# The fill of a two-attention pipeline, written out as an order of its own

## Chip, core, metric

The kernel runs on 1 core of one Trainium2 chip. The metric is the device time of one execution in microseconds; three executions are timed, and a fourth is profiled.

## What is computed

Eight images of 32 x 32 tokens with 256 channels pass through two residual attention blocks, each behind a group normalisation over 32 groups of channels:

```python
def reference(x, w_qkv, w_proj, b_proj, Wq, Wk, Wv, gamma):
    ...
    x = x + _L0_conv_ref(_gn(x), L0_conv_w_qkv, L0_conv_w_proj, L0_conv_b_proj)
    x = x + _L1_conv_ref(_gn(x), L1_conv_Wq, L1_conv_Wk, L1_conv_Wv, L1_conv_gamma)
    return x
```

`_L0_conv_ref` is attention inside windows of 32 tokens with 8 heads of width 32, then a 256 x 256 projection and a bias. `_L1_conv_ref` is attention over all 1024 tokens of an image, with `energy = k q^T` of inner width 32, a softmax over the keys, and `gamma * (attn v)`.

## The kernel before

The first block is called the local stage (names that begin with `a_`), the second the global stage (`b_`). Products that need more than half precision are made of three float16 matmuls (`split3`, lines 253 to 255), so weights and activations exist as a high and a low part (`a_nh` and `a_nl`, `b_nh` and `b_nl`, `v_h` and `v_l`).

Each engine has one program, written by hand in the order in which it runs, and semaphores join them. `pa` is four PSUM banks of 512 floats for the local stage, `pb` four banks for the global stage. A step `i` of the pipeline has two halves, `first(i, b, o, m, f)` and `second(i, b, o, m, f)`. The flags say which image's work exists: `f` is the front of the local stage of image i+2, `m` the rest of the local stage of image i+1, `b` the global attention of image i, `o` the output of image i-1. The program runs `first(-2)`, `second(-2)`, then `all_steps`, which runs the steps from -1 up, with steps 2 to 4 as a loop.

The local stage of one image goes like this. The image is loaded (`load`) and turned by TensorE (`transposes`), ScalarE copies it out (`copy_T`), VectorE takes statistics (`stats`), TensorE averages over groups (`group_mean`, `group_var`), GpSimd makes the factors (`rstd`), ScalarE and GpSimd make `a_nh` and `a_nl`. TensorE projects q and k (`a_project_qk`) and v (`a_project_v`). SyncE spreads k onto the diagonal of `diag` by 8 DMAs (`k_spread`, line 333). TensorE makes scores (`a_scores`); VectorE subtracts maxima (`a_maximum`, lines 874 and 879), ScalarE exponentiates (`a_exponential`, line 714), VectorE sums rows (`a_row_sum`, lines 884 and 886), GpSimd multiplies (`a_probabilities`, line 1083), VectorE turns blocks (`a_transpose`, line 892), SyncE spreads them into the same `diag` by 8 DMAs (`p_spread`, line 343), and TensorE makes the outputs (`a_output`, line 491). ScalarE and VectorE split them into `before_turn` (`a_out_high`, `a_out_low`, line 896), SyncE regroups that by 16 DMAs (`a_regroup`, line 321), and TensorE projects (`a_projection`); VectorE adds the result to the image (`a_residual`, line 905) and so has `x1`.

The global stage of an image turns `x1`, normalises it (`b_norm_split` on VectorE, lines 860 and 862), projects q and k, and copies them into `q_stack` and `k_stack` by 4 DMAs (`b_stacks`, lines 307 to 310). For each of 8 row tiles TensorE makes an energy (`b_energy`, line 539) and VectorE a maximum (`b_maximum`, line 925). With all maxima split (`b_max_split`, line 932), the second half `second(i)` makes the transposed energies (`b_energy_T`, line 557), their exponentials (line 749) and the value projection (`b_project_v`, `b_v_high`, `b_v_low`), between the matmuls of the local stage of image i+2 and the end of that of image i+1. The weights are scaled at the start: a maximum of each matrix, a turn and a sum on TensorE (lines 656 and 658), then `weights_high` and `weights_low`.

An engine runs strictly in its written order: what stands behind a waiting instruction waits too. The DMAs of SyncE stand in one such order as well.

## Time and profile before

| what | value |
|---|---|
| time, median of 3 | 690.84 us (688.51 to 690.97) |
| the profiled execution's own time | 689.47 us |
| its span | 687.7 us |
| TensorE busy | 593.7 us (86%) |
| VectorE busy | 473.2 us (69%) |
| ScalarE busy | 349.5 us (51%) |
| GpSimd busy | 196.9 us (29%) |
| mean granted TensorE clock | 0.945 |

The span is the time from the first to the last instruction of the profiled execution; what lies around it, 1.8 us here, is in the time too. Times within the trace are counted from the span's start. The granted clock is given as a share of full speed: 1.00 is 2.4 GHz and 0.50 is 1.2 GHz.

### The profile page before, as it was taken

How to read it: one execution, taken by the hardware profiler on the slowest of the kernel's cores; microseconds unless marked ns; L12 is line 12 of the kernel's file. 1: busy time of each engine (PE TensorE's matmuls, PEld its weight loads, DVE VectorE, ACT ScalarE, POOL GpSimd, SP SyncE). 2: the span in 40 equal slices, each digit the busy share in tenths (PEclk: the TensorE clock that was granted, in tenths of full speed). 3: DMA queues.
4: the chain of work that ended last, by engine and by line, in shares of the span. 5: the costliest groups of instructions: out<-in, count | busy, mean ns of one | idle time of the engine just before them, and what ended most of it. 6: DMA issues, size and time to landing. Idle time of an engine off the chain costs nothing.

```text
span 687.7 us, 15145 instructions
## 1 busy us (share of the span) xinstructions
PE 593.7 (86%) x5859; PEld 429.9 (63%) x5859; DVE 473.2 (69%) x765; ACT 349.5 (51%) x486; POOL 196.9 (29%) x194
## 2 busy tenths in 40 slices
PE   2475587689999999999999999999999999649987
PEld 2254265346877677757775777668776767327756
DVE  4445246868886878687868788688868794664562
ACT  2522425097518852686348652875278513651363
POOL 5602221132046023513342314420460342001203
PEclk9795798599999999999999999999999999879999
DMA  5042132212332332243042323224223132201101
GB/s 160 0 124 62 43 83 82 62 38 64 108 74 66 78 93 71 63 108 93 23 107 76 84 61 92 68 57 112 68 68 82 33 74 64 72 1 39 49 0 62
DMA packets 40308, 47.53 MB, mean 69 GB/s; under 512 B 6848, under 2 KB 32320, under 8 KB 40256
## 3 DMA queue, kind: packets, MB, share of 16 engines
q1 hardware_dynamic: 36960, 43.47, 24.0%
q10 hardware_dynamic: 3296, 3.34, 1.4%
q8 instruction: 35, 0.57, 0.4%
q14 instruction: 17, 0.14, 0.1%
HBM read 10.09 MB, written 8.39 MB: 27 GB/s over the span
## 4 chain that ended last, share of the span: by engine, by line
PE 64%; DVE 16%; ACT 6%; issue 5%; SPq 4%; DMA 3%; POOL 1%; ACTq 0%; DVEq 0%; POOLq 0%
PE pb L253 9%; PE pb L254 8%; PE pb L255 8%; PE pa L253 7%; PE pa L255 6%; PE pa L254 6%; PE pa L491 4%; DVE max_neg L925 4%; PE pb L557 4%; PE pa L464 3%; PE pb L539 3%; SPq L321 3%; DVE ast L827 2%; PE pa L393 2%; PE pb L393 2%
## 5 line engine op out<-in xcount | busy, mean ns | idle before, releaser
L253 PE MATMUL pb<-v_h,e_h 128*128 128x257 f16 x464 | 127.5, 275 | 0.0
L255 PE MATMUL pb<-v_h,e_l 128*128 128x257 f16 x464 | 126.5, 273 | 0.0
L254 PE MATMUL pb<-v_l,e_h 128*128 128x257 f16 x464 | 126.1, 272 | 0.0
L925 DVE TENSOR_REDUCE max_neg<-pb 128x1 f32<-128x1024 f32 x64 | 77.5, 1211 | 55.6 <-PE pb L539 55.1
L940 DVE TENSOR_TENSOR e_l<-e,e_h 128x1024 f16<-128x1024 f32 x64 | 77.8, 1223 | 17.1 <-ACT e L749 15.5
L758 ACT ACTIVATE qk_h<-pb,y_fac 128x256 f32<-128x256 f32 x58 | 27.5, 474 | 109.9 <-DVE y_fac L947 109.6
L1097 POOL TENSOR_TENSOR y<-qk_h,y 128x256 f32<-128x256 f32 x64 | 46.3, 727 | 118.1 <-ACT qk_h L758 118.0
L749 ACT ACTIVATE e<-pb,f_energy 128x1024 f32<-128x1024 f32 x64 | 71.3, 1114 | 16.1 <-PE pb L557 16.1
L1078 POOL TENSOR_TENSOR xb<-xin,bias 128x2048 f32<-128x2048 f32 x8 | 36.7, 4588 | 125.9 <-DVE x L905 125.9
L1083 POOL TENSOR_TENSOR before_turn<-before_turn,a_rinv 128x1024 f32<-128x1024 f32 x16 | 30.6, 1912 | 128.3 <-DVE a_rinv L886 128.3
L253 PE MATMUL pa<-a_nh,wqkv_h 128*128 128x512 f16 x128 | 49.9, 389 | 13.1 <-DVE before_turn L896 7.3
L748 ACT ACTIVATE e_h<-pb,f_energy 128x1024 f16<-128x1024 f32 x40 | 44.5, 1113 | 20.2 <-PE pb L557 20.1
L253 PEld LDWEIGHTS pb<-v_h,e_h 128*128 128x128 f16 x464 | 45.7, 99 | 13.7 <-issue 1.7
L254 PEld LDWEIGHTS pb<-v_l,e_h 128*128 128x128 f16 x464 | 45.7, 98 | 11.9
L539 PE MATMUL pb<-q_stack,k_stack 96*128 96x512 f16 x128 | 40.4, 398 | 14.2 <-DVE max_neg L925 12.8
L693 ACT ACTIVATE a_nh<-a_xT,anb,ar 128x512 f16<-128x512 f32 x32 | 25.7, 803 | 48.2 <-POOL anb L1060 48.2
L254 PE MATMUL pa<-a_nl,wqkv_h 128*128 128x512 f16 x128 | 49.7, 388 | 0.0
L255 PE MATMUL pa<-a_nh,wqkv_l 128*128 128x512 f16 x128 | 49.5, 387 | 0.0
L255 PEld LDWEIGHTS pb<-v_h,e_l 128*128 128x128 f16 x464 | 44.7, 96 | 6.9
L557 PE MATMUL pb<-k_stack,q_stack 98*128 98x512 f16 x128 | 38.9, 385 | 10.9 <-ACT e L749 9.5
L1071 POOL TENSOR_TENSOR a_nl<-a_xT,a_nh 128x512 f16<-128x512 f32 x32 | 37.1, 1158 | 18.7 <-ACT a_xT L695 18.7
L253 PE MATMUL pa<-wp_h,turned 128*128 128x256 f16 x128 | 35.9, 281 | 2.3 <-DMA turned<-before_turn 2.3
(136 smaller groups left out, 1373.4 us busy)
## 6 DMA issues: line engine op xcount, KB each, us to landing
xin<-in_x SPq DMA_DIRECT2D x16, 512.0 KB, 4.6
diag<-qkT SPq DMA_DIRECT2D x64, 128.0 KB, 2.3
diag<-turned SPq DMA_DIRECT2D x64, 128.0 KB, 2.4
turned<-before_turn SPq DMA_DIRECT2D x128, 64.0 KB, 2.0
out<-y SPq DMA_DIRECT2D x24, 256.0 KB, 2.1
out<-y ACTq DMA_DIRECT2D x8, 256.0 KB, 2.1
q_stack<-qk_hl SPq DMA_DIRECT2D x8, 128.0 KB, 2.3
k_stack<-qk_hl SPq DMA_DIRECT2D x8, 128.0 KB, 2.4
```

What stands on the lines that cost most here:

```text
L253: nc.tensor.matmul(out_ap, lh, rh, start=start, stop=False)
L254: nc.tensor.matmul(out_ap, lh, rl, start=False, stop=False)
L255: return nc.tensor.matmul(out_ap, ll, rh, start=False, stop=stop)
L539: last = nc.tensor.matmul(pb[:, c, :], k_stack[0:96, it * P:(it + 1) * P], q_stack[0:96, c * CHUNK:(c + 1) * CHUNK], start=True, stop=True)
L557: last = nc.tensor.matmul(pb[:, c, :], q_stack[0:98, jt * P:(jt + 1) * P], k_stack[0:98, c * CHUNK:(c + 1) * CHUNK], start=True, stop=True)
L748: nc.scalar.activation(e_h[:, jt, :], src, ACT.Exp, scale=f_energy[:, 0:1])
L749: nc.scalar.activation(e32[:, jt % 2, :], src, ACT.Exp, scale=f_energy[:, 0:1]).then_inc(b_exp, 1)
L925: nc.vector.tensor_reduce(max_neg[:, it:it + 1], pb[:, 0:2, :].rearrange("p a n -> p (a n)"), X, ALU.max, negate=True).then_inc(b_max, 1)
L940: nc.vector.tensor_tensor(e_l[:, jt, :], e32[:, jt % 2, :], e_h[:, jt, :], ALU.subtract).then_inc(b_el, 1)
L1071: nc.gpsimd.tensor_tensor(a_nl[:, ct, cols], a_xT[:, ct, cols], a_nh[:, ct, cols], ALU.subtract).then_inc(n_["a"]["nl"], 1)
L1078: nc.gpsimd.tensor_tensor(xb[:], xin[:], bias[:].unsqueeze(1).broadcast_to([P, TILES, CH]), ALU.add).then_inc(a_xb, 1)
L1097: nc.gpsimd.tensor_tensor(y[:, it, :], y_part[:, it % 2, :], y[:, it, :], ALU.add).then_inc(b_y, 1)
```

## The change

The fill, that is all work up to the maxima of image 0's energies, is no longer `first(-2)`, `second(-2)`, `first(-1)`, `second(-1)` and `first(0)`, but a list of its own on each engine. `all_steps` then begins with `second(0)`. In the new list

- image 0 is loaded ahead of `w_proj` and the global stage's weights on SyncE's queue, and it is turned ahead of the weights' maxima on TensorE;
- image 1 is turned through banks 2 and 3 of `pb` (`turn_bank`), and its group means and variances stand there (`group_bank`), so that it can be turned while image 0's scores are not yet done; its q, k, v and scores stand between the stages of image 0;
- image 0's projection goes to `pb` (`proj_bank`);
- the value projection of image 0's global stage, with its high and low parts, stands ahead of and between the first energies and no longer in `second(0)`;
- `memset` of `diag` comes first on GpSimd, and the small ones later.

```diff
-            for i in range(-1, 2):
-                peeled(first, i)
-                peeled(second, i)
+            peeled(second, 0)
+            peeled(first, 1)
+            peeled(second, 1)
...
+        def turn_bank(k, b, j):
+
+            return pa[:, j, :] if k == "a" and not image(b, 1) else pb[:, 2 + j % 2, :]
+
+        def group_bank(k, b, which):
+
+            if k == "b":
+                return pb[:, 2 + which, 0:CT]
+            return pb[:, 2 + which, 384:384 + CT] if image(b, 1) else pa[:, 1 + 2 * which, 384:384 + CT]
+
+        def proj_bank(b, j):
+
+            return pb[:, 2 + j % 2, :] if image(b, 0) else pa[:, 2 + j % 2, :]
...
+            load(0)
             sp.dma_start(wp_f, w_proj.rearrange("(a p) n -> p a n", p=P)).then_inc(s_wp, 16)
...
-            load(0)
-            sp.wait_ge(s_pool, 6)
-            second(-2, False, False, False, True)
+            load(1)
+            sp.wait_ge(s_pool, 2)
+            sp.nop(nofuse=True)
+            k_spread(0, 0)
+            k_spread(0, 1)
+            p_spread(0, 0)
+            p_spread(0, 1)
+            k_spread(1, 0)
+            k_spread(1, 1)
+            a_regroup(0)
+            load(2)
+            p_spread(1, 0)
+            p_spread(1, 1)
+            b_stacks(0)
             all_steps(sp, first, second)
...
+            transposes("a", 0, range(4))
+            group_mean("a", 0)
             pe.wait_ge(s_wmax, 1)
...
+            group_var("a", 0)
...
-            first(-2, False, False, False, True)
 
             pe.wait_ge(s_ready, 1)
-            second(-2, False, False, False, True)
+            a_project_qk(0, 0, range(4))
+            transposes("a", 1, (0, 1))
+            a_project_qk(0, 1, (0, 1))
+            transposes("a", 1, (2, 3))
+            a_project_qk(0, 1, (2, 3))
+            a_project_v(0, (0, 1))
+            group_mean("a", 1)
+            a_project_v(0, (2, 3))
+            group_var("a", 1)
+            a_scores(0)
+            a_project_qk(1, 0, range(4))
+            a_project_qk(1, 1, range(4))
+            a_output(0, True, 0)
+            a_output(0, True, 1)
+            a_project_v(1, range(4))
+            a_scores(1)
...
+            a_projection(0, True, range(4))
+            transposes("b", 0, range(4))
+            group_mean("b", 0)
+            group_var("b", 0)
...
+            for c in range(CHUNKS):
+                b_project_qk(0, True, c)
+            transposes("a", 2, range(4))
+            b_project_v(0, (0, 1))
+            b_energy(0, 0, True)
+            b_project_v(0, (2,))
+            b_energy(0, 1, True)
+            b_project_v(0, (3,))
+            b_energy(0, 2, True)
+            group_mean("a", 2)
+            a_output(1, True, 0)
+            b_energy(0, 3, True)
+            group_var("a", 2)
+            a_output(1, True, 1)
+            for it in range(4, 8):
+                b_energy(0, it, True)
...
             def second(i, b, o, m, f):
-                if b: b_project_v(i, (0,))
+                if b and not image(i, 0): b_project_v(i, (0,))
                 if b: b_max_rows(i)
...
+            a_exponential(0, 0)
+            a_exponential(0, 1)
...
+            a_exponential(1, 0)
+            copy_T("b", 0, range(4))
+            normalise("b", 0)
+            a_exponential(1, 1)
+            b_qk_high(0)
...
+            weight_maximum(slice(0, 1))
+            stats("a", 0)
+            weight_maximum(slice(1, 5)).then_inc(s_wmax, 1)
...
+            a_residual(0, range(4))
+            a_maximum(1, 1)
+            stats("b", 0)
+            group_mean("b", 0)
+            a_row_sum(1, 0)
+            group_scale("b", 0)
+            a_row_sum(1, 1)
+            b_norm_split(0)
+            a_transpose(1, 0)
+            a_transpose(1, 1)
+            b_qk_low(0)
...
```

Three places of the order are needed later. The first is VectorE, from the variance of image 0's global normalisation (`be`, `bve`) to its high and low parts. Before the change:

```order
L845 TENSOR_TENSOR be<-be,bmv 128x2 [waits bn_sq]
L850 TENSOR_SCALAR bve<-pb 128x2 [waits bn_gv]
L860 CAST b_nh<-b_xT 128x512 [waits bn_xn]
L862 TENSOR_TENSOR b_nl<-b_xT,b_nh 128x512 [waits bn_nh]
...
L874 TENSOR_REDUCE a_rmax<-pa 128x32 [waits a_s]
L879 TENSOR_TENSOR before_turn<-pa,a_rmax 128x1024 [waits a_ox,a_max]
L914 SCALAR_TENSOR_TENSOR qk_hl<-qk_h,masks,pb 128x512 [waits b_qkh] x2
```

With the change:

```order
L948 TENSOR_TENSOR be<-be,bmv 128x2 [waits bn_sq]
L987 TENSOR_REDUCE a_rsum<-before_turn 128x32 [waits a_exp]
L989 RECIPROCAL a_rinv<-a_rsum 128x32 [waits a_sum]
L953 TENSOR_SCALAR bve<-pb 128x2 [waits bn_gv]
L987 TENSOR_REDUCE a_rsum<-before_turn 128x32 [waits a_exp]
L989 RECIPROCAL a_rinv<-a_rsum 128x32 [waits a_sum]
L963 CAST b_nh<-b_xT 128x512 [waits bn_xn]
L965 TENSOR_TENSOR b_nl<-b_xT,b_nh 128x512 [waits bn_nh]
...
L995 STREAM_TRANSPOSE turned<-before_turn 128x1024 [waits a_y,a_prob] x2
L1017 SCALAR_TENSOR_TENSOR qk_hl<-qk_h,masks,pb 128x512 [waits b_qkh] x2
```

Image 1's two row sums (`a_rsum`) moved ahead of the split of image 0's normalised tokens, and its two block turns (`turned`) stand between that split and `qk_hl`.

The second is ScalarE over the same stretch, from the copies of the turned `x1` (`b_xT<-pb`) on. Before:

```order
L680 ACTIVATE b_xT<-pb 128x512 [waits bn_tr] x4
L710 ACTIVATE v_tok<-pb 128x512 [waits a_o,a_v] x3
L695 ACTIVATE b_xT<-b_xT,bnb,br 128x512 [waits bn_nb]
L695 ACTIVATE b_xT<-b_xT,bnb,br 128x512
...
L729 ACTIVATE qk_h<-pb 128x512 [waits b_qk] x2
L714 ACTIVATE before_turn<-before_turn 128x1024 [waits a_sub] x2
```

With the change:

```order
L795 ACTIVATE before_turn<-before_turn 128x1024 [waits a_sub]
L761 ACTIVATE b_xT<-pb 128x512 [waits bn_tr] x4
L776 ACTIVATE b_xT<-b_xT,bnb,br 128x512 [waits bn_nb]
L776 ACTIVATE b_xT<-b_xT,bnb,br 128x512 x3
L795 ACTIVATE before_turn<-before_turn 128x1024 [waits a_sub]
L810 ACTIVATE qk_h<-pb 128x512 [waits b_qk] x2
```

Image 1's second exponential (`before_turn<-before_turn`) moved from behind `qk_h` to between the normalisation of image 0 and `qk_h`.

The third is SyncE's queue, from the regrouping of image 0 (`turned<-before_turn`) to that of image 1; `diag<-qkT` is a k spread, `diag<-turned` a spread of probabilities. Before:

```order
L321 DMA turned<-before_turn 32x2x512 [waits a_ol]
L321 DMA turned<-before_turn 32x2x512 x15
L333 DMA diag<-qkT 32x2x512 [waits a_ke,a_o]
...
L297 DMA xin<-in_x 128x4x256 [waits an_tr,a_xb] x2
L307 DMA q_stack<-qk_hl 64x1024 [waits b_qkl]
L308 DMA k_stack<-qk_hl 64x1024
L309 DMA q_stack<-qk_hl 32x1024
L310 DMA k_stack<-qk_hl 32x1024
L343 DMA diag<-turned 32x1024 [waits a_pt,a_s]
```

With the change:

```order
L338 DMA turned<-before_turn 32x2x512 [waits a_ol]
L338 DMA turned<-before_turn 32x2x512 x15
L314 DMA xin<-in_x 128x4x256 [waits an_tr,a_xb] x2
L360 DMA diag<-turned 32x1024 [waits a_pt,a_s]
L360 DMA diag<-turned 32x1024 x3
L360 DMA diag<-turned 32x1024 [waits a_pt,a_s]
L360 DMA diag<-turned 32x1024 x3
L324 DMA q_stack<-qk_hl 64x1024 [waits b_qkl]
L325 DMA k_stack<-qk_hl 64x1024
L326 DMA q_stack<-qk_hl 32x1024
L327 DMA k_stack<-qk_hl 32x1024
```

The 8 k spreads of image 1 went ahead of the regrouping of image 0, and the 8 spreads of image 1's probabilities went from behind the 4 stack transfers to ahead of them.

## Rows read from the trace of the kernel before

**Rows 1.** Windows: length, busy of PE, PEld, DVE, ACT, POOL, clock, DMA.

```profile
116.00:150.00 34.00, 24.21 (x221) 15.10 (x222) 23.11 (x32) 15.52 (x21) 11.57 (x12) 0.71 0.18 42
150.00:190.00 40.00, 39.31 (x386) 28.45 (x385) 32.32 (x49) 26.92 (x38) 6.65 (x4) 1.00 0.33 87
```

**Rows 2.** Chain of waits that ended last: start, length, what.

```profile
3.52 6.83 DMA gam<-in_L_conv_gamma
...
87.15 1.99 DMA turned<-before_turn
```

**Rows 3.** Timeline, ScalarE: start, length, instruction, idle before it.

```profile
22.43 0.81 ACT L693 ACTIVATE a_nh<-a_xT,anb,ar 128x512 f16<-128x512 f32 x1 [5.79 <-POOL anb L1060]
...
106.47 1.51 ACT L695 ACTIVATE b_xT<-b_xT,bnb,br 128x512 f32<-128x512 f32 x2
...
115.89 1.06 ACT L714 ACTIVATE before_turn<-before_turn 128x1024 f32<-128x1024 f32 x1 [2.63 <-DVE before_turn L879]
```

**Rows 4.** Timeline, TensorE.

```profile
26.80 0.59 PE L253 MATMUL pa<-a_nh,wqkv_h 128*128 128x512 f16 x1 [5.76 <-POOL a_nl L1071]
...
45.20 3.70 PE L464 MATMUL pa<-diag,qkT 128*32 128x128 f32 x128 [0.99 <-DMA diag<-qkT]
...
89.18 0.28 PE L253 MATMUL pa<-wp_h,turned 128*128 128x256 f16 x1 [2.06 <-DMA turned<-before_turn]
...
97.89 1.04 PE L393 MATMUL pb<-ident,x 128*128 128x128 f32 x8
...
119.44 1.06 PE L539 MATMUL pb<-q_stack,k_stack 96*128 96x512 f16 x2
...
131.35 3.64 PE L491 MATMUL pa<-diag,v_tok 128*32 128x128 f32 x64
...
136.57 1.96 PE L491 MATMUL pa<-diag,v_tok 128*32 128x128 f32 x64 [0.57 <-DMA diag<-turned]
...
140.47 0.59 PE L539 MATMUL pb<-q_stack,k_stack 96*128 96x512 f16 x2 [1.41 <-DVE max_neg L925]
...
145.92 0.60 PE L557 MATMUL pb<-k_stack,q_stack 98*128 98x512 f16 x2 [1.10 <-ACT k_stack L740]
...
158.80 0.60 PE L557 MATMUL pb<-k_stack,q_stack 98*128 98x512 f16 x2
```

**Rows 5.** Timeline, VectorE.

```profile
95.57 0.75 DVE L905 SCALAR_TENSOR_TENSOR x<-pa,f_proj,xb 128x512 f32<-128x512 f32 x1 [1.50 <-PE pa L255]
...
102.76 0.16 DVE L850 TENSOR_SCALAR bve<-pb 128x2 f32<-128x2 f32 x1 [0.70 <-PE pb L405]
...
109.07 0.69 DVE L862 TENSOR_TENSOR b_nl<-b_xT,b_nh 128x512 f16<-128x512 f32 x1
...
114.63 1.22 DVE L879 TENSOR_TENSOR before_turn<-pa,a_rmax 128x1024 f32<-128x1024 f32 x1
115.78 1.21 DVE L884 TENSOR_REDUCE a_rsum<-before_turn 128x32 f32<-128x1024 f32 x1
117.02 0.35 DVE L886 RECIPROCAL a_rinv<-a_rsum 128x32 f32<-128x32 f32 x1
...
142.57 0.17 DVE L932 SCALAR_TENSOR_TENSOR max_hl<-max_neg,max_hl 128x8 f16<-128x8 f32 x1
...
146.11 1.21 DVE L896 TENSOR_TENSOR before_turn<-pa,before_turn 128x1024 f16<-128x1024 f32 x1
```

**Rows 6.** Timeline, SyncE's queue: issues.

```profile
56.99 5.04 SPq L343 DMA_DIRECT2D diag<-turned  x8
77.51 10.23 SPq L321 DMA_DIRECT2D turned<-before_turn  x16
...
115.73 0.59 SPq L310 DMA_DIRECT2D k_stack<-qk_hl  x1
```

**Rows 7.** Timeline, GpSimd and VectorE at the same time.

```profile
193.35 1.91 POOL L1083 TENSOR_TENSOR before_turn<-before_turn,a_rinv 128x1024 f32<-128x1024 f32 x1 [1.97 <-DVE a_rinv L886]
...
194.45 0.82 DVE L947 TENSOR_TENSOR y_fac<-y_inv,f_out 128x1 f32<-128x1 f32 x1
```

177 lines of the change are left out of this document (125 added, 52 removed).

## The prediction, made blind

> **What bounds the kernel now.** I read the windows first, then the chain of waits, then the timelines of the engines up to 190 us. From 150 us on TensorE is busy 39.31 of 40 us at full clock [rows 1], so there the kernel is bound by TensorE and an offset gained or lost before is carried to the end. From 116 to 150 us it is busy 24.21 of 34 us at a mean clock of 0.71 [rows 1]: there, and earlier, latency bounds it. The change rewrites just this part, so the question is when TensorE reaches a place from which its work is the same in both programs. I take the projection of image 1 (`a_projection(1)`): before, TensorE comes to it when the sixth transposed energy is done, at 158.80 + 0.45 = 159.25 us [rows 4], and its input has landed by then, at about 159.1 us: the low part of the outputs ends at 147.32 us [rows 5], then 16 DMAs are issued and the last lands, 11.7 us together (from 77.51 [rows 6] to 89.18 [rows 4]).
>
> **The new order, walked in steps.** Each step below adds durations of rows; "before" is the same event in the trace.
>
> *Start.* TensorE's first instruction waits for the last constant, at 3.52 + 6.83 = 10.35 us [rows 2]; the first projection comes at 26.80 us [rows 4]. The image loaded first does not lift this gate, and its turn and the weights' scale still share one chain: VectorE now has four weight maxima behind the image's statistics and ahead of the scale. I take the length from gate to projection as it was (16.45 us; bounds 2 less and 2 more). But 1 MB of image now stands ahead in the DMA engines; I add 0.9 us (bounds 0 and 2.8). First projection: 27.7 us.
> The Trainium skill, "DMA: Bandwidth & Descriptors", section on queues, rings and completion order, says that each DMA engine takes turns between the queues that have work; the constants are on another queue than the image, so by this rule nothing would be added, and by a strict first come, first served all of the image's transfer. No run here shows which.
>
> *Image 0's scores.* Image 1 is turned between the projections: 2 x 1.04 us [rows 4]. Scores start at 45.20 + 0.9 + 2.1 = 48.2 (before 45.20).
>
> *Image 0's local attention.* First half of the scores at 50.05; maxima and differences 4 x 1.21 (as the rows of lines 879 and 884 [rows 5]) to 55.0. The exponentials, 1.06 us each [rows 3], stand behind image 1's normalisation on ScalarE (8 x 0.71, from 49.2) and so start at 54.9. Two row sums with reciprocals, 1.56 each [rows 5], to 59.1; two k copies of image 1 (1.35, as two other copies of their kind) to 60.4; two block turns 2.5 to 62.9. The spread of probabilities, 8 issues in 5.04 us [rows 6], starts at 61.7 behind the first turn, its last DMA lands at 68.6, and half the outputs takes 1.96 us at high clock or 3.64 at low [rows 4]. TensorE has worked until 2.3 us before, so I take 1.96: 70.5 us.
>
> *Regrouping.* The queue now issues image 1's 8 k spreads first, 5.04 us, to 75.6. High and low part of the outputs (1.91 + 2.4 us) are hidden by that. Regrouping starts at 75.65 (before 77.51 [rows 6]): 1.9 sooner. The projection of image 0: 87.3 (before 89.18 [rows 4]).
>
> *x1.* TensorE has idled 6 us and starts at low clock, which costs about 1.6 us on 48 matmuls of 0.11; the last residual ends at 95.0 (before 95.57 + 0.75 = 96.3 [rows 5]): 1.3 sooner. Image 1's projections, values and scores are already behind us here; their work is what the change takes off this stretch.
>
> *Variance of the global norm.* Now VectorE does image 1's second maximum and difference first (2.4, to 97.4), then statistics (2.85), the averages (1.3, four VectorE products of 2 columns and two small matmuls), then a row sum of 1.56, and only then `bve`: 103.2 (before 102.92 [rows 5]). The gain is gone.
>
> *Its high and low parts.* Factors 1.05, four normalisations of 0.75 (two in 1.51 [rows 3]) to 107.3. `b_norm_split` stands behind image 1's second row sum, which waits for an exponential that ScalarE runs only behind that normalisation: 1.06 + 1.56 to 109.9. At that moment GpSimd starts its product of 1.92 us. In the rows a VectorE product of 128x1, else 0.16 us, took 0.82, from 194.45 to 195.27, and the GpSimd product beside it ran from 193.35 to 195.26 [rows 7]: VectorE was held until GpSimd ended. I take it that casts and differences with two SBUF inputs are held alike: 1.5 us (bounds 0 and 1.9). End of the split: 115.7 (before 109.07 + 0.69 = 109.76 [rows 5]): 5.9 later.
> The Trainium skill, "SBUF — State Buffer", section on the two separate sides, calls the shared port pair an exclusive lock held for a whole instruction; by it a cast that comes first would instead hold GpSimd, for 0.4 us. The trace agrees as far as the one row goes.
>
> *First energy.* Before, 109.76 to 119.44 [rows 4]. Now image 1's block turns come first on VectorE (2.45), and on SyncE's queue 8 spreads stand ahead of the 4 stack transfers. The spreads start at 116.95 and occupy the queue for 5.04 us [rows 6] to 122.0; the last of the stack issues starts 1.85 later and lands in 2.0 (before: issued at 115.73 [rows 6]). First energy: 126.0, 6.6 later. `qk_hl` is ready at 119.5 and waits.
>
> *Energies to the split maxima.* Before 119.44 to 142.74 [rows 4, 5], 23.3 us, much at low clock. Between the maxima VectorE now has two `v_l` (1.4), half the statistics (1.6) and the group mean (0.8), no longer row sum and block turns. With a cycle of 2.0 us at high clock (0.59 + 1.41 [rows 4]) and the waits for both output halves it comes to 20.6 us; with energies of 1.06 and output halves of 3.64 [rows 4] to 27. The value projections keep TensorE busy for some microseconds at the start of it, so I take 22.0: split maxima at 148.0 (before 142.74), 5.3 later.
>
> *Second half, step 0.* Before, the first transposed energy came 3.2 us behind the split, since v copies and the output's high part stood ahead of the row copy on ScalarE; now 1.8: 149.8 (before 145.92 [rows 4]), 3.9 later. Of the four value projections taken out (1.31 us each, 5.2 together), two lay in that wait, one lies under an exponential (1.11 twice), and one, 1.3 us, was in TensorE's own path. So the sixth transposed energy ends 11.9 us on, at 161.7. The regrouping of image 1: low parts end at 150.45, all landed 11.7 later, 162.2. This is later than TensorE. `a_projection(1)`: 162.2 against 159.25, **2.9 us later**. From there both programs do the same, bound by TensorE, so 2.9 us is what is left at the end.
>
> Other moves cost nothing: `diag` cleared first on GpSimd ends before the constants land; the small memsets lie under ScalarE's copies; image 2's load ends 20 us before its turn.
>
> **Sum.** 689.47 (the profiled execution) + 2.9 = 692.4. The profiled execution lies 1.4 us under the median of the three timed ones (690.84); the mean of all four is 690.0, and I set the forecast against that: 690.0 + 2.9 = 692.9. What a measurement of this kernel can tell from no change is about 0.5%, 3.45 us.
>
> **Rivals.**
> *The energies run at low clock* (0.2). For: the clock of this stretch before, 0.71 [rows 1], and now a wait of 4 us for the stack transfers ahead of it. Price: 27 instead of 22 us, +5, and +1.7 if image 0's output half is slow too: 695 to 700.
> *The steps cancel* (0.17). The constants land as before (-0.9), the GpSimd product holds nothing (-1.5), the stretch runs at high clock (-1.4): -0.9 in all, 689.1. Against: all three have to hold.
> *The maxima hide VectorE's other work* (0.13), the faster side. If `v_l`, statistics and averages fit into the 1.4 us in which VectorE waits in each cycle, energies to split is 8 x 2.0 + 0.5 = 16.5 us, the split comes at 142.5, the regrouping lands at 156.7, and TensorE arrives at 156.2: -2.6, and with the constants unmoved -3.5, 686.5. It decides from a stretch under 18.5 us. Against: three waits for TensorE's averages and output halves stand in that stretch in written order.
> *Image first does take the gate away*: an earlier first constant would shift all by as much; the gate's own DMA is untouched, so I give it a part of the last rival only.
>
> **How the numbers follow.** Forecast (offset of +1 to +5, 691 to 695): 0.5. Of it 40% lie above 3.45 us. Slower by over 0.5%: 0.2 + 0.2 = 0.40. Faster by over 0.5%: 0.13, the last rival with room for a step that I overlooked. The same: 0.47. Range: from 687.5, between the two rivals below, to 698, in the low clock's; about 0.1 lies outside on each side. The likeliest one's own range is 691 to 695.
>
> **What would show it.** In the new trace: first projection near 27.7 us; regrouping of image 0 issued near 75.7; first b_nh cast near 110, a held cast or difference beside a GpSimd product; the q and k stack DMAs issued behind 8 probability spreads, near 122; first energy near 126; split maxima near 148; TensorE waiting for `turned` ahead of image 1's projection, near 162. Wrong would be: a first energy before 121, an energies stretch under 19 us, or a clock that stays low into `second(0)`.

## The result

| | kernel before | changed kernel |
|---|---|---|
| time, median of 5 | 688.51 us (688.17 to 690.97) | 694.38 us (693.66 to 696.15) |
| ratio to before | | 1.0082, 95% interval 1.0062 to 1.0103 |
| profiled execution's own time, span | 689.47 us, 687.7 us | 696.15 us, 694.4 us |
| TensorE, VectorE busy | 593.7 us, 473.2 us | 593.8 us, 470.4 us |
| mean granted TensorE clock | 0.945 | 0.953 |

The change makes the kernel 0.8% slower. In a second comparison on another chip it was 1.0107 [1.0081, 1.0133] of before (`e10_changed_again`, below). By the medians its cost was 5.9 us in the first comparison and 7.5 us in the second. The forecast was 692.9 us, that is +2.9 us.

The windows of the changed kernel, with the columns of [rows 1]:

```profile
116.00:150.00 34.00, 23.37 (x224) 14.29 (x224) 20.20 (x31) 13.21 (x20) 7.09 (x9) 0.80 0.19 44
150.00:190.00 40.00, 36.93 (x327) 23.11 (x328) 29.34 (x45) 24.78 (x31) 6.06 (x5) 0.89 0.30 80
```

Against [rows 1] the first stretch has about as much TensorE work (23.37 against 24.21 us), at a better clock (0.80 against 0.71). The loss shows in the second: 36.93 busy of 40 us against 39.31, and a clock of 0.89 against 1.00. The stretch in which latency bounds the kernel has grown longer, past 150 us.

TensorE's timeline of the changed kernel shows where it comes to each place (start, length, instruction, idle before it and what ended that):

```profile
25.79 0.58 PE L270 MATMUL pa<-a_nh,wqkv_h 128*128 128x512 f16 x1 [6.29 <-POOL a_nl L1218]
...
88.57 0.37 PE L270 MATMUL pb<-wp_h,turned 128*128 128x256 f16 x1 [5.69 <-DMA turned<-before_turn]
...
115.93 0.59 PE L270 MATMUL pb<-b_nh,wqk_h 128*128 128x512 f16 x1 [11.61 <-DVE b_nl L965]
...
128.70 1.04 PE L583 MATMUL pb<-q_stack,k_stack 96*128 96x512 f16 x2 [2.90 <-DMA k_stack<-qk_hl]
...
146.11 1.01 PE L583 MATMUL pb<-q_stack,k_stack 96*128 96x512 f16 x2 [1.41 <-DVE max_neg L1028]
...
151.28 1.01 PE L590 MATMUL pb<-ident_h,max_hl 128*2 128x128 f16 x8 [1.73 <-DVE max_hl L1035]
153.39 1.04 PE L601 MATMUL pb<-k_stack,q_stack 98*128 98x512 f16 x2 [1.11 <-ACT k_stack L821]
...
156.78 1.06 PE L601 MATMUL pb<-k_stack,q_stack 98*128 98x512 f16 x2
...
166.43 0.61 PE L601 MATMUL pb<-k_stack,q_stack 98*128 98x512 f16 x2
```

The same places, before, predicted, and measured:

| event | before | predicted | measured |
|---|---|---|---|
| first projection | 26.80 | 27.7 | 25.79 |
| projection of image 0 (L270 <- turned) | 89.18 | 87.3 | 88.57 |
| last residual ends (`x1`) | 96.3 | 95.0 | 97.5 |
| `bve` ends | 102.92 | 103.2 | 105.4 |
| high and low parts of image 0 end | 109.76 | 115.7 | 117.8 |
| first energy | 119.44 | 126.0 | 128.70 |
| maxima split, end | 142.74 | 148.0 | 151.22 |
| first transposed energy | 145.92 | 149.8 | 153.39 |
| projection of image 1 | 159.25 | 162.2 | 166.87 |

From there the offset only travels. SyncE's regrouping of later images was issued at 219.91 and, for the last image, at 583.51 us before; in the changed kernel at 227.73 and 591.22, so +7.8 for the first of them and still +7.7 five images later. The last image's first energy comes at 632.87 against 626.03: 0.9 us is given back in the last steps, where TensorE waits again, and the span ends 6.7 us later.

VectorE of the changed kernel, over the stretch in which the offset grows:

```profile
105.32 0.10 DVE L953 TENSOR_SCALAR bve<-pb 128x2 f32<-128x2 f32 x1
110.41 1.22 DVE L987 TENSOR_REDUCE a_rsum<-before_turn 128x32 f32<-128x1024 f32 x1 [5.00 <-ACT before_turn L795]
...
111.94 0.36 DVE L963 CAST b_nh<-b_xT 128x512 f16<-128x512 f32 x1
112.34 2.27 DVE L965 TENSOR_TENSOR b_nl<-b_xT,b_nh 128x512 f16<-128x512 f32 x1
...
117.72 2.37 DVE L995 STREAM_TRANSPOSE turned<-before_turn 128x1024 f32<-128x1024 f32 x2
...
121.88 0.75 DVE L1017 SCALAR_TENSOR_TENSOR qk_hl<-qk_h,masks,pb 128x512 f16<-128x512 f16 x1 [1.17 <-ACT qk_h L810]
```

ScalarE of the changed kernel at the same time:

```profile
109.34 1.04 ACT L795 ACTIVATE before_turn<-before_turn 128x1024 f32<-128x1024 f32 x1
...
121.25 0.60 ACT L810 ACTIVATE qk_h<-pb 128x512 f16<-128x512 f32 x1 [1.96 <-PE pb L272]
```

and GpSimd:

```profile
112.10 1.96 POOL L1230 TENSOR_TENSOR before_turn<-before_turn,a_rinv 128x1024 f32<-128x1024 f32 x1 [3.76 <-DVE a_rinv L989]
```

VectorE has nothing to do for 5.00 us ahead of 110.41: it stands at the second row sum of image 1, which waits for the exponential of 109.34 that ScalarE runs behind image 0's normalisation. The first chunk of image 0 has been normalised since about 107.2, and its cast, behind that row sum, comes at 111.94. Then `b_nl` of 112.34 takes 2.27 us, where the other three take 0.69: it begins when GpSimd's product (112.10 to 114.06) already runs, and it ends 0.55 us after that product.

SyncE's queue of the changed kernel:

```profile
69.75 6.26 SPq L350 DMA_DIRECT2D diag<-qkT  x8
76.12 10.93 SPq L338 DMA_DIRECT2D turned<-before_turn  x16
...
119.50 5.17 SPq L360 DMA_DIRECT2D diag<-turned  x8
124.78 0.53 SPq L324 DMA_DIRECT2D q_stack<-qk_hl  x1
...
153.61 10.25 SPq L338 DMA_DIRECT2D turned<-before_turn  x16
```

The 8 spreads of image 1's probabilities hold the queue from 119.50 to 124.7. `qk_hl` is complete at 122.63, and its first transfer is issued at 124.78. TensorE waits 11.61 us for `b_nl` (115.93) and then 2.90 for the stacks (128.70).

### The profile page after: what moved, and what is told of

Read it like the earlier page. It is cut to its first block, busy times and chain, and to the rows that moved or that the text cites. A ratio compares the mean times of both kernels' runs of the same rounds, so it can differ in the third digit from the quotient of the medians.

```text
span 694.4 us, 15142 instructions
## 1 busy us (share of the span) xinstructions
PE 593.8 (86%) x5859; PEld 428.5 (62%) x5859; DVE 470.4 (68%) x765; ACT 349.0 (50%) x486; POOL 197.8 (28%) x194
## 4 chain that ended last, share of the span: by engine, by line
PE 65%; DVE 15%; ACT 7%; issue 5%; SPq 4%; DMA 3%; POOL 1%; ACTq 1%; DVEq 0%; POOLq 0%
PE pb L270 9%; PE pb L271 9%; PE pb L272 9%; PE pa L270 6%; PE pa L271 6%; PE pa L272 6%; PE pb L601 4%; DVE max_neg L1028 4%; PE pa L535 4%; PE pb L583 3%; PE pa L502 3%; ACT e L830 2%; PE pa L425 2%; PE pb L425 2%; DVE a_rsum L987 2%
## 5 line engine op out<-in xcount | busy, mean ns | idle before, releaser
L270 PE MATMUL pb<-v_h,e_h 128*128 128x257 f16 x464 | 127.4, 275 | 0.0
L270 PE MATMUL pa<-a_nh,wqkv_h 128*128 128x512 f16 x128 | 50.1, 391 | 9.1 <-POOL a_nl L1218 9.1
L270 PEld LDWEIGHTS pb<-v_h,e_h 128*128 128x128 f16 x464 | 45.7, 99 | 13.6 <-issue 1.4
L583 PE MATMUL pb<-q_stack,k_stack 96*128 96x512 f16 x128 | 39.5, 391 | 16.8 <-DVE max_neg L1028 12.5
L601 PE MATMUL pb<-k_stack,q_stack 98*128 98x512 f16 x128 | 40.3, 397 | 10.9 <-ACT e L830 9.5
L270 PE MATMUL pb<-wv_h,b_nh 128*128 128x256 f16 x128 | 35.6, 278 | 0.0
```

What stands on the lines that cost most here:

```text
L270: nc.tensor.matmul(out_ap, lh, rh, start=start, stop=False)
L583: last = nc.tensor.matmul(pb[:, c, :], k_stack[0:96, it * P:(it + 1) * P], q_stack[0:96, c * CHUNK:(c + 1) * CHUNK], start=True, stop=True)
L601: last = nc.tensor.matmul(pb[:, c, :], q_stack[0:98, jt * P:(jt + 1) * P], k_stack[0:98, c * CHUNK:(c + 1) * CHUNK], start=True, stop=True)
```

## The experiments

Each is the changed kernel with one edit, unless it says otherwise, and was executed 4 to 12 times. The ratio is to the kernel before on the same chip, whose medians were 689.5 to 690.1 us there (688.51 in the first comparison). The last three columns are starts on TensorE in the one profiled execution ("rows of maxima" is `b_max_rows`, which follows the split). The two traces of the unaltered changed kernel show how far one program's starts differ: 1.2 us at the first energy, but only 0.02 at the rows of maxima and 0.2 at the sixth transposed energy. These two columns tell more than the first.

| kernel | time, us | ratio [95%] | first energy | rows of maxima | sixth transposed energy |
|---|---|---|---|---|---|
| kernel before | 688.51 | 1 | 119.44 | 142.80 | 158.80 |
| changed | 694.38 | 1.0082 [1.0062, 1.0103] | 128.70 | 151.28 | 166.43 |
| the same again | 697.11 | 1.0107 [1.0081, 1.0133] | 129.88 | 151.30 | 166.22 |
| `e1_sum_late` | 697.18 | 1.0113 [1.0087, 1.0138] | 127.39 | 149.83 | 164.43 |
| `e2_stacks_first` | 695.69 | 1.0071 [1.0049, 1.0093] | 127.70 | 149.66 | 164.06 |
| `e3_both` | 689.06 | 0.9986 [0.9967, 1.0006] | 122.00 | 144.57 | 158.55 |
| `e5_turn_between` | 693.57 | 1.0055 [1.0031, 1.0078] | 127.64 | 149.67 | 164.01 |
| `e4_load_last` | 698.79 | 1.0140 [1.0108, 1.0173] | 129.43 | 150.84 | 165.60 |
| `e6_v_back` | 696.90 | 1.0104 [1.0080, 1.0129] | 128.41 | 150.68 | 165.41 |
| `e7_filler` | 693.76 | 1.0052 [1.0035, 1.0070] | 127.81 | 149.72 | 162.86 |
| `e8_chain_first` | 688.07 | 0.9972 [0.9960, 0.9983] | 118.94 | 141.99 | 156.05 |
| `e9_chain_filler` | 684.49 | 0.9936 [0.9910, 0.9961] | 117.67 | 139.40 | 152.53 |
| `e11_regroup_first` | 689.30 | 0.9997 [0.9977, 1.0017] | 118.92 | 142.68 | 157.16 |
| before, `e12_before_filler` | 687.54 | 0.9969 [0.9953, 0.9985] | 120.66 | 144.41 | 159.15 |

### Two gates ahead of the first energy: e1, e2, e3

The theory: the first energy is late because image 1's work stands ahead of image 0's at two places, the row sum on VectorE (with its exponential on ScalarE) and the spreads on SyncE's queue.

`e1_sum_late` moves the first, `e2_stacks_first` the second, `e3_both` both:

```diff
 # e1, ScalarE
-            a_exponential(1, 1)
             b_qk_high(0)
+            a_exponential(1, 1)
 # e1, VectorE
-            a_row_sum(1, 1)
             b_norm_split(0)
+            b_qk_low(0)
+            a_row_sum(1, 1)
             a_transpose(1, 0)
             a_transpose(1, 1)
-            b_qk_low(0)
 # e2, SyncE
+            b_stacks(0)
             p_spread(1, 0)
             p_spread(1, 1)
-            b_stacks(0)
```

> Image 1's second exponential and row sum stand behind qk_high and qk_low of image 0; SyncE's queue is as in the changed kernel. Theory (chain and queue together): the split of image 0's normalised tokens ends near 111.6 us instead of 117.8 and qk_hl is ready near 115.6 instead of 122.6, but the stack transfers stay behind 8 spreads of probabilities that now wait for a later row sum, so the first energy moves from 128.7 to about 128 and the time falls by under 1 us against the changed kernel (694.4). Rival (the row sum is the whole cause): the first energy at about 120 to 122 and the time 5 to 7 us lower, near 688.

> Only SyncE's queue changes: the 4 stack transfers of image 0 stand ahead of the 8 spreads of image 1's probabilities. Theory: qk_hl is ready at 122.6, so the first stack issue is at 122.7 instead of 124.8 and the first energy at about 126.6 instead of 128.7; the spreads land near 132.5, still ahead of image 1's outputs at 136.9. Time 2 us lower than the changed kernel, near 692.4. Rival (the queue is the whole cause): 5 us lower or more.

> Both edits of the two runs before. Theory: qk_hl ready near 115.6, first energy near 119.6 (before the change 119.4), that is about 9 us sooner than in the changed kernel, although the two edits alone give under 1 and 2 us; split maxima near 142.5; time 7 to 9 us below the changed kernel, 685.5 to 687.5, at or a little under the kernel before. Rival (low clock of TensorE in the stretch is what costs): the first energy moves, but the split maxima stay beyond 147 and the time above 690.

Each edit alone took 1.0 to 1.3 us off the first energy, hardly more than the 1.2 by which two traces of the changed kernel differ, and 1.8 to 2.4 us off the sixth transposed energy. Their ratios, 1.0113 and 1.0071, show no gain clear of noise: the first lies above and the second below the changed kernel's own two. Both together took 6.7 us off the first energy and 7.7 to 7.9 off the sixth transposed energy, and the time came back to that of before. It was expected under that, at 685.5 to 687.5 us, with a first energy at 119.6 and not 122.0; `e8_chain_first` below takes up what was left. The rival expected of it, rows of maxima still late at low clock, did not come about. The rows of `e1_sum_late`, SyncE and then TensorE, say why the first alone does so little:

```profile
118.34 5.02 SPq L360 DMA_DIRECT2D diag<-turned  x8
123.47 0.53 SPq L324 DMA_DIRECT2D q_stack<-qk_hl  x1
```

```profile
127.39 1.04 PE L583 MATMUL pb<-q_stack,k_stack 96*128 96x512 f16 x2 [9.56 <-DMA k_stack<-qk_hl]
```

`qk_hl` was complete at 114.89 there, 7.7 us sooner than in the changed kernel, but the stack transfers stand behind spreads that now wait for the late row sum and turns: the queue comes to them at 123.47, and TensorE waits 9.56 us. In `e2_stacks_first` the transfers go at 123.78, as soon as `qk_hl` is there (123.31), but `qk_hl` is late. In `e3_both` VectorE and the queue are both free. VectorE, and then SyncE's queue:

```profile
108.18 1.27 DVE L963 CAST b_nh<-b_xT 128x512 f16<-128x512 f32 x1 [1.95 <-ACT b_xT L776]
...
116.86 0.75 DVE L1017 SCALAR_TENSOR_TENSOR qk_hl<-qk_h,masks,pb 128x512 f16<-128x512 f16 x1 [1.22 <-ACT qk_h L810]
```

```profile
118.08 0.53 SPq L324 DMA_DIRECT2D q_stack<-qk_hl  x1
```

`qk_hl` ends at 117.61 and its first transfer goes at 118.08. VectorE's rows show the held instruction once more: the cast of 108.18 takes 1.27 us instead of 0.42, beside GpSimd's product of image 1's first half.

### The GpSimd product: e5

`e5_turn_between` puts image 1's first block turn between the second row sum and the high and low parts, so that it is the turn that runs when the product begins:

```diff
             a_row_sum(1, 1)
-            b_norm_split(0)
             a_transpose(1, 0)
+            b_norm_split(0)
             a_transpose(1, 1)
```

> Image 1's first block turn stands on VectorE between its second row sum and the split of image 0's normalised tokens, beside GpSimd's product. Theory of the lock (VectorE's casts and two-input differences are held while GpSimd's product runs, a turn is not): the turn takes its 1.2 us, and the first cast and difference together take under 2.2 us instead of 2.7; the split ends within 0.7 us of 117.8. The first four spreads leave SyncE's queue from 113.3 on and no longer block the stacks, so the first energy comes at 126.5 to 127.5 instead of 128.7; time 1 to 2 us lower than the changed kernel. Rival (no lock; the 2.27 us difference was something else): the first difference takes 2.2 us again.

VectorE of this kernel:

```profile
112.53 1.19 DVE L995 STREAM_TRANSPOSE turned<-before_turn 128x1024 f32<-128x1024 f32 x1
113.64 1.25 DVE L963 CAST b_nh<-b_xT 128x512 f16<-128x512 f32 x1
114.92 0.69 DVE L965 TENSOR_TENSOR b_nl<-b_xT,b_nh 128x512 f16<-128x512 f32 x1
```

and SyncE's queue:

```profile
114.27 9.34 SPq L360 DMA_DIRECT2D diag<-turned  x8
123.72 0.53 SPq L324 DMA_DIRECT2D q_stack<-qk_hl  x1
```

The turn is not held (1.19 us, as ever), but the cast behind it is, 1.25 instead of 0.42 us. Cast and difference together take 1.94 us, in the changed kernel 2.63, so 0.7 us of the hold is saved and 0.8 remains. The first energy came 1.1 us sooner and the sixth transposed energy 2.4; the ratio is 1.9 to 3.6 us below the changed kernel's two, with an interval that meets that of the first.

These gains are not the shorter hold's. The turn now stands ahead of the split, so the split ended at 118.80 us, 1.0 later than in the changed kernel, where I had expected it within 0.7, and `qk_hl` was complete at 123.35, 0.7 later. What came sooner is the queue: the first four spreads left from 114.27 on (the row merges them with the other four, 120.09 to 123.61), so the stack transfers went at 123.72 instead of 124.78. Of the 2.4 us at the sixth transposed energy, 0.8 are clock: the third transposed energy came 2.03 us behind the second (2.87 in the changed kernel). So the rows show a hold of about 1.5 us in the changed kernel (2.63 us against 0.42 + 0.69), a part and not the cause of the loss; what it is worth in the time, this edit does not show.

### The start and the value projections: e4, e6

`e4_load_last` moves `load(0)` back behind the weights on SyncE's queue. `e6_v_back` takes image 0's value projections, with their high and low parts, out of the fill and puts them back into `second(0)`:

```diff
 # e4, SyncE
-            load(0)
             sp.dma_start(wp_f, w_proj.rearrange("(a p) n -> p a n", p=P)).then_inc(s_wp, 16)
...
+            load(0)
 # e6, TensorE
-            b_project_v(0, (0, 1))
             b_energy(0, 0, True)
-            b_project_v(0, (2,))
             b_energy(0, 1, True)
-            b_project_v(0, (3,))
...
-                if b and not image(i, 0): b_project_v(i, (0,))
+                if b: b_project_v(i, (0,))
```

> Image 0's load goes back behind the weights on SyncE's queue, all else as changed. In the changed kernel the first turn starts at 10.38 us with the last constant, and the first projection at 25.79. Theory (the load's place is worth at most what the image lands later than the constant): the first turn starts at 11 to 12.5, the first projection at 26.5 to 28, the time 0.5 to 2 us higher. Rival (the place of the load is worth nothing, since the constant gates both): first turn at 10.4 and no change.

> The value projection of image 0's global stage and its high and low parts go back into second(0); all else as changed. Theory (moving them was worth about one microsecond): first energy unchanged near 128.7, split maxima 1 to 2 us sooner, the first transposed energy at the same distance from the split as before the change (3.2 us) instead of 2.2, the sixth transposed energy about 1.3 us further behind the first; the time within 1.5 us of the changed kernel. Rival (taking 5.2 us of TensorE work from second(0) paid in full and hid a larger loss): the time rises by 4 to 5 us, near 699.

TensorE's start in `e4_load_last`:

```profile
12.07 3.65 PE L425 MATMUL pa<-ident,xin 128*128 128x128 f32 x16 [12.07 <-DMA xin<-in_x]
...
27.45 0.58 PE L270 MATMUL pa<-a_nh,wqkv_h 128*128 128x512 f16 x1 [6.30 <-POOL a_nl L1218]
```

With the image behind the weights its turn waits for the image until 12.07 us, and the first projection comes at 27.45 instead of 25.79. So loading the image first is worth 1.7 us at its place. Whether it is worth anything at the end is open. The time rose to 1.0140, 2 to 4 us above the changed kernel, where 0.5 to 2 was expected, but its interval meets that of the changed kernel's second comparison, and the trace does not carry the delay: `x1` was there at 97.75 against 97.5, because the low clock of image 0's projection lasted 2.7 us instead of 5.7, and the sixth transposed energy came at 165.60, ahead of the changed kernel's 166.43 and 166.22. That profiled execution, at 695.16 us, was the quickest of its four.

`e6_v_back` shows both sides of the value projections. Among the energies they cost nothing that can be told: from the first energy to the rows of maxima it takes 22.27 us without them and 22.58 with them, and the rows of maxima came 0.6 us sooner where 1 to 2 was expected. In `second(0)` they lengthen the way from the first to the sixth transposed energy to 12.87 us, as before (12.88 from [rows 4]), against 13.04 in the changed kernel, where the first two steps ran at low clock. The times, 1.0104 against 1.0082 and 1.0107, do not differ: this move neither makes the loss nor hides it.

### The clock: e7

`e7_filler` adds to the changed kernel matmuls of `wqkv_h` with itself, 128x512, whose results nobody reads, in the stretches in which TensorE idles (4 more stand behind the rows of maxima, and a wait for `b_vl` ahead of the last four energies; both are left out here):

```diff
+            def filler(bank, n):
+                for _ in range(n):
+                    nc.tensor.matmul(bank, wqkv_h[:, 0, 0:P], wqkv_h[:, 0, 0:CHUNK], start=True, stop=True)
...
             a_scores(1)
+            pe.wait_ge(a_ve, 8)
+            filler(pb[:, 0, :], 24)
...
+            filler(pb[:, 0, :], 48)
             for c in range(CHUNKS):
                 b_project_qk(0, True, c)
...
+            pe.wait_ge(b_qkl, 2)
+            filler(pb[:, 0, :], 24)
             b_energy(0, 0, True)
...
             for it in range(4, 8):
                 b_energy(0, it, True)
+                filler(pb[:, 2, :], 4)
```

> The changed kernel with TensorE matmuls added whose results nobody reads, in its idle stretches: 24 ahead of image 0's projection, 48 ahead of the projection to global q and k, 24 ahead of the first energy, 4 behind each of the last four energies and behind the rows of maxima. Theory (the low clock costs a part of the loss): granted clock near 1.00 from 84 us on; last residual of image 0 ends about 2 us sooner, the last three energy cycles take 2.0 instead of 2.4 us, the first transposed energies 2.8 and 1.8 apart instead of 3.4 and 2.9; the time 3 to 6 us below the changed kernel. Rival (low clock is covered by other waits): under 1 us. If the added matmuls are too many and delay a step, its start shows it.

The windows of this kernel, with the columns of [rows 1]:

```profile
110.00:120.00 10.00, 10.00 (x60) 5.83 (x59) 9.32 (x13) 2.94 (x6) 1.96 (x1) 1.00 0.12 27
...
150.00:160.00 10.00, 9.11 (x45) 3.50 (x43) 6.21 (x6) 7.54 (x9) 0.00 (x0) 1.00 0.28 70
```

The clock is 1.00 from 110 to 120 and from 150 to 160 us, where the changed kernel had 0.50 and 0.55. `qk_hl` was there at 119.5 us instead of 122.6, but the queue still stood at the spreads, so the first energy came only 0.9 us sooner. The last stack transfer was issued 2.0 us sooner (124.62 against 126.62) but took 3.15 us to land instead of 2.03. The energies and the first transposed energies then gained 2.7 us more (sixth at 162.86). The time is 1.0052, 2 to 4 us under the changed kernel by the ratios, with an interval that meets that of the first comparison; 3 to 6 us were expected. Low clock is thus a part of the loss, 3.6 us at the sixth transposed energy where the order of `e3_both` is worth 7.9, and what it gains ahead of the first energy is hidden as long as the queue is the gate.

### Image 0's chain first: e8

`e8_chain_first` is `e3_both` with two more of image 1's operations moved behind image 0's:

```diff
             a_residual(0, range(4))
-            a_maximum(1, 1)
             stats("b", 0)
             group_mean("b", 0)
-            a_row_sum(1, 0)
             group_scale("b", 0)
+            a_maximum(1, 1)
             b_norm_split(0)
+            a_row_sum(1, 0)
             b_qk_low(0)
```

> As the run with both edits, and on VectorE image 1's second maximum stands behind the variance of image 0's global norm, its first row sum behind the split of the normalised tokens. Theory (what stands in image 0's chain is late by what it takes, 2.4 and 1.5 us): variance near 103.3 instead of 106.1, first cast 0.4 us instead of 1.27 since no GpSimd product runs beside it, first energy near 119 instead of 122.0; time 2 to 3 us below the run with both edits, near 686. Rival (the chain is held elsewhere, by TensorE's turns and clock): no change against it.

TensorE of this kernel:

```profile
118.94 0.61 PE L583 MATMUL pb<-q_stack,k_stack 96*128 96x512 f16 x2 [1.33 <-DMA k_stack<-qk_hl]
...
156.05 0.60 PE L601 MATMUL pb<-k_stack,q_stack 98*128 98x512 f16 x2
...
157.78 0.28 PE L270 MATMUL pa<-wp_h,turned 128*128 128x256 f16 x1 [1.13 <-DMA turned<-before_turn]
```

`bve` started at 102.89 us, 3.3 sooner than in `e3_both` (106.14) and 2.4 sooner than in the changed kernel (105.32), the first cast was not held (0.42 us), and the first energy came at 118.94, 3.1 us before that of `e3_both` and 9.8 before the changed kernel's. The time is 0.9972 [0.9960, 0.9983], faster than before. Here TensorE does wait for the regrouping ahead of image 1's projection, 1.13 us: the wait that I had forecast for the changed kernel appears when TensorE is early enough.

### The new order again, with the clock held, and one step more: e10, e9, e11

`e10_changed_again` is the changed kernel unaltered. `e9_chain_filler` is `e8_chain_first` with extra matmuls at the places of `e7_filler`, 22, 20, 18 and 4 (the last behind each of the last four energies and behind the rows of maxima; its expectation names that place wrongly). `e11_regroup_first` is `e8_chain_first` with image 1's k spreads behind image 0's regrouping, and what hangs on them moved back:

```diff
 # e11, SyncE
+            a_regroup(0)
             k_spread(1, 0)
             k_spread(1, 1)
-            a_regroup(0)
 # e11, TensorE
-            a_scores(1)
...
             group_var("b", 0)
+            a_scores(1)
```

> The changed kernel once more, so that it stands beside the two next ones on one chip. Expected: a ratio of 1.007 to 1.009 to the kernel before, as measured first (1.0082), so about 5.5 us above it, and 6 to 7.5 us above the level of the order that moves image 1's work behind image 0's (688.07 us when it was measured). If that order's gain was the chip's and not the order's, the distance here is under 4 us.

> The order that moves image 1's work behind image 0's and puts the stack transfers first, plus TensorE matmuls of which nobody uses the result, in the stretches in which it idles (22 ahead of image 0's variance, 20 ahead of the first low part, 18 ahead of the first energy, 4 ahead of image 0's projection quarters). Theory that low clock still costs in this fill: the first energy comes at about 117.5 us instead of 118.9, the first three transposed energies are 2.8 and 1.8 us apart, and the time is 0.5 to 2 us under that order's own level of about 688 us; it is held to that because the regrouped outputs of image 1 land at about 158.5 and TensorE's wait for them, 1.1 us, grows. Rival, that only latencies of VectorE, ScalarE and DMA bound the fill: the same time within 0.5 us, or longer, because the added matmuls stand in front of real ones.

> The same order, and moreover the regrouping of image 0 stands ahead of the k spreads of image 1 on SyncE's queue, with all that hangs on those spreads moved back: image 1's scores behind image 0's variance on TensorE, its maxima, exponentials and row sums one place later on VectorE and ScalarE. Theory, that each microsecond taken off image 0's chain ahead of the first energy is a microsecond off the time as long as image 1's own chain is covered: the regrouping starts at about 74 us instead of 77.0, image 0's projection comes at 86.5, bve at about 100.4, the first energy at about 116.5, and the time is 1 to 2.5 us under that order's level, about 686 us. Rival, that image 1's chain is then the later one: its outputs wait for its spreads by more than 2 us among the energies, its regrouping lands as late as before, the wait of TensorE ahead of image 1's projection grows to about 3 us, and the time stays at 688.

The distance from `e9_chain_filler` to the changed kernel, on one chip, is 12.6 us. The extra matmuls gave more than expected. TensorE in `e9_chain_filler`:

```profile
82.16 4.92 PE L701 MATMUL pb<-wqkv_h 128*128 128x512 f16 x22
89.20 0.27 PE L270 MATMUL pb<-wp_h,turned 128*128 128x256 f16 x1 [2.12 <-DMA turned<-before_turn]
...
100.83 6.16 PE L701 MATMUL pb<-wqkv_h 128*128 128x512 f16 x20
...
117.67 0.60 PE L583 MATMUL pb<-q_stack,k_stack 96*128 96x512 f16 x2
...
152.53 0.61 PE L601 MATMUL pb<-k_stack,q_stack 98*128 98x512 f16 x2
153.40 0.28 PE L270 MATMUL pa<-wp_h,turned 128*128 128x256 f16 x1 [0.27 <-DMA turned<-before_turn]
```

Image 0's projection now starts at full clock (0.27 us a matmul from the first one), `bve` came at 101.01 against 102.89, the first energy 1.3 us sooner, the rows of maxima 2.6 and the sixth transposed energy 3.5; the spans differ by 4.6 us. I had expected the regrouping to hold it back, but the low part of the outputs stands behind the split on VectorE and moved with it: the regrouping was issued at 141.72 instead of 144.32, and TensorE waited 0.27 us (153.40).

The counts are not the best ones. The first low part of image 0 was ready at 104.62 us, but TensorE was at the 20 extra matmuls until 107.0. The last stack transfer, issued at 113.33, landed at about 115.4 (2.0 us), but TensorE stood at the 18 extra matmuls (113.79) until the first energy at 117.67. So in both places matmuls that nobody reads held real ones, by 2.4 and about 2.2 us. No run has fewer of them.

`e11_regroup_first` started the regrouping at 74.72 and image 0's projection at 86.47, as expected; the first energy was to come at 116.5 and came at 118.92. TensorE of this kernel:

```profile
86.47 0.37 PE L270 MATMUL pb<-wp_h,turned 128*128 128x256 f16 x1 [10.88 <-DMA turned<-before_turn]
...
100.48 5.37 PE L502 MATMUL pa<-diag,qkT 128*32 128x128 f32 x128
```

and VectorE of the same kernel:

```profile
103.59 1.23 DVE L977 TENSOR_REDUCE a_rmax<-pa 128x32 f32<-128x1024 f32 x1 [2.99 <-PE pa L502]
...
105.99 0.42 DVE L963 CAST b_nh<-b_xT 128x512 f16<-128x512 f32 x1
```

Image 1's scores, now at 100.48, ran 5.37 us at low clock instead of 3.70, and VectorE's maximum of image 1 (103.59), which stands ahead of the first cast, waited 2.99 us for them: the 2.5 us won at `bve` (100.44) were lost there, to 105.99 against 105.36. This is the changed kernel's fault in small: work of image 1 ahead of a ready instruction of image 0. The ratio is 0.9997, 1.7 us behind `e8_chain_first` by the ratios, with intervals that just meet; 1 to 2.5 us ahead of it was expected. The rival named for it, outputs of image 1 that wait for their spreads and a longer wait ahead of its projection, is not what the rows show: TensorE took that projection at 157.60 us without a wait.

### Is it the order or the clock: e12

`e12_before_filler` puts the extra matmuls into the kernel before, 26 behind the turn of image 1, 30 ahead of image 1's projections, 18 behind image 0's global projections, and 4 behind each energy of image 0:

```diff
             def first(i, b, o, m, f):
+                if at(i, 0): filler(pb[:, 2, :], 18)
...
+                    if at(i, -1) and it == 1: filler(pb[:, 2, :], 26)
                     if b and it >= 1: b_energy(i, (0, 2, 3)[it - 1], m)
+                    if at(i, 0) and it >= 1: filler(pb[:, 2, :], 4)
...
             def second(i, b, o, m, f):
+                if at(i, -1): filler(pb[:, 2, :], 30)
```

> The kernel before, with TensorE matmuls of which nobody uses the result in the idle stretches of its own fill: 26 behind the turn of image 1 (its low clock in image 0's outputs), 30 ahead of image 1's projections, 18 behind image 0's global projections, and 4 behind each of image 0's energies. It asks whether the gain of the reordered fill with such matmuls (684.49 us, 0.9936 of before) is the clock's alone or needs the new order. Theory, that the two are separate and add: the old order gains where its rows show low clock on its own chain, which is image 0's output halves (3.64 instead of 1.96 us each, partly under a DMA wait), and the energies (five cycles of 2.42 instead of 2.0 us and one output half), so the first energy comes 1 to 2 us sooner, the split maxima 3 to 5 us sooner than 142.74, and the time is 2.5 to 4.5 us under before, ratio 0.9935 to 0.9965; the new order is then worth little beside the clock. Rival, that the old order's stretch is bound by VectorE's other work between the maxima (9.37 us busy of 10 from 120 to 130): the split comes less than 1.5 us sooner, the time stays within 1 us of before, and the gain at full clock needs the new order.

The windows of this kernel, and then its TensorE:

```profile
60.00:90.00 30.00, 22.81 (x217) 12.04 (x215) 7.23 (x16) 10.31 (x14) 5.54 (x6) 1.00 0.28 67
116.00:150.00 34.00, 26.41 (x260) 15.38 (x259) 25.85 (x35) 14.99 (x22) 11.59 (x12) 1.00 0.21 48
```

```profile
120.66 0.61 PE L539 MATMUL pb<-q_stack,k_stack 96*128 96x512 f16 x2
...
125.26 0.59 PE L539 MATMUL pb<-q_stack,k_stack 96*128 96x512 f16 x2 [2.00 <-DVE max_neg L937]
...
137.54 1.95 PE L491 MATMUL pa<-diag,v_tok 128*32 128x128 f32 x64 [1.81 <-DMA diag<-turned]
...
159.15 0.60 PE L557 MATMUL pb<-k_stack,q_stack 98*128 98x512 f16 x2
```

The clock is 1.00 where it was 0.71 [rows 1], and the time is 0.9969 [0.9953, 0.9985] of before, 2.0 us by the medians. Neither expectation fits well: the lower end of one was 2.5 us and the upper end of the other 1. The profiled execution began 1.6 us late (first projection at 28.41 against 26.80), and counted from there the rows of maxima came no sooner than before, the sixth transposed energy 1.3 us sooner (won behind the rows of maxima, from which the first transposed energy came in 1.87 instead of 3.12 us), and the span ended 1.8 us sooner. That the energies gave nothing fits the rival's reason, VectorE's other work between the maxima (2.00 us of wait at 125.26), together with an output half that waits for its spreads (1.81 us at 137.54). So the clock alone gives the old order 2 us, the better order alone gives 2 us (`e8_chain_first`), and the two together 4.4 us by the ratio and 5.1 by the medians (`e9_chain_filler`). These three were measured on three chips, each against the kernel before on its own.

## Why the prediction was right, and where its sum was short

The sign, the place and the mechanism were right: the offset arises ahead of the first energy, from image 1's row sum ahead of the split of image 0 on VectorE, and from the 8 spreads ahead of the stack transfers on SyncE's queue, and it is carried unchanged through the part that TensorE bounds. `e3_both` shows both, since the loss vanished with these two moves, and `e1_sum_late` and `e2_stacks_first` show that neither is to be seen alone. The size was half or less: 2.9 us for a measured 5.9 and 7.5. The last step, a TensorE that waits for the regrouping of image 1, was wrong.

Two things were luck. The measured 694.38 us lies within the forecast's own 691 to 695 only because the kernel before came out at 688.51 there and not at the 690.0 that I had added to; the offset, 5.9 us, lies above its +1 to +5. And I gave more to a change of under 0.5% (0.47) than to a slower kernel (0.40), and it was 0.8%. One of the three signs that I had named for being wrong did appear, a clock that stays low into `second(0)`: 0.55 from 150 to 160 us. Step by step:

**Start.** The 0.9 us for a megabyte of image ahead of the constants was not there: the gate opened at 10.38 us against 10.40. The way from the gate to the first projection was 1.0 us shorter than before, not as long. The scores started at 45.25 us and not at 48.2, because before the change they had waited 0.99 us for their DMA [rows 4], and I added the 2.1 us of image 1's turns to a start that had this wait in it.
The Trainium skill, "DMA: Bandwidth & Descriptors", section on queues, rings and completion order, has each DMA engine take turns between the queues with work. The trace agrees: the constants on their other queue lost nothing.

**Image 0's local stage and the regrouping.** The output halves ran at high clock (1.96 us each), as taken. They ended at 69.66 us against 70.5, so of the 2.95 us by which the scores were early 0.8 were left: the last spread of probabilities took 3.48 us from its issue to landing (64.09 to 67.57), where I had taken 2.5. The regrouping was issued at 76.12 against a forecast of 75.65, because the k spreads took 6.26 us and not 5.04, and it took 10.93 instead of 10.23.

**x1.** This is the first term that was mis-sized. TensorE had idled 5.69 us and ran at low clock for 5.7 us, which is 27 of the 48 matmuls at 0.21 us apart instead of 0.11. That is 2.8 us and not the 1.6 in the forecast: from the start of the projection to the last residual 8.9 us instead of the forecast 7.7. With the 1.3 us from the queue, `x1` was 1.2 us later than before instead of 1.3 sooner, a miss of 2.5 us.

**The split.** The row sum that waits, 1.06 + 1.56 us, and the product that holds VectorE, 1.5 us, were right: 2.27 against 0.69 is 1.58. The Trainium skill, "SBUF — State Buffer", section on the two separate sides, has the shared pair held for a whole instruction by whichever starts first. The trace agrees: the cast began before the product and took its 0.36 us, the difference began after it and had to wait. From `bve` to the end of the split it was 12.4 us against a forecast of 12.5.

**First energy.** 10.9 us behind the split, forecast 10.3; the spreads took 5.17 and the issues as forecast. But I had counted `qk_hl` as ready at 119.5 and waiting. `b_project_qk` began at low clock after 11.61 us of idle, so `qk_h` came at 118.69 and 121.25, and `qk_hl` at 122.6, only 2.2 us ahead of the queue. It did not set the time here, but it left less to be won by `e2_stacks_first`.

**The energies.** 22.5 us against 22.0, with the first and the last two of the eight at low clock (1.04 us at 128.70, 1.01 at 146.11). The rival of 27 us did not come about. The clock was down mostly behind them: 0.55 from 150 to 160 us, so the first three transposed energies were 3.39 and 2.87 us apart (153.39, 156.78, 159.65) instead of 3.05 and 1.80 before. These 1.4 us cancelled the value projection that was taken out, 1.25 us, which I had booked as gain. With 0.4 us at the rows of maxima, also at low clock, this is the second term that was mis-sized, 2.0 us in all.

**The wait ahead of image 1's projection.** I took the regrouping to be the last to arrive, 162.2 against TensorE's 161.7. It had landed at about 165.3 and TensorE came at 166.87, so there was no wait; the offset is TensorE's own, +7.6 us. This term cost nothing in the sum, because the two were half a microsecond apart in the forecast, but the reason given was wrong. `e8_chain_first` has the wait (1.13 us), with TensorE 10 us sooner.

The misses along the chain: 2.5 us at `x1`, -0.4 from there to the end of the split, 0.6 to the first energy, 0.5 in the energies, 0.4 to the first transposed energy, 1.6 to the sixth. They sum to 5.2 us, the distance from TensorE's forecast arrival (161.7) to the measured one (166.87). About 3.5 of the 5.2 are TensorE at low clock behind idle time where I had taken it at high clock, or for a shorter while, or had not looked; 1.2 are the queue's longer issues. `e7_filler`, with the clock at 1.00, has its sixth transposed energy 3.6 us sooner, which fits.

The rivals: "the steps cancel" had one of its three conditions (the constants), and "the maxima hide VectorE's other work" failed at the energies, 22.5 us and not under 18.5. The forecast's range held, since it reached to 698.
